# Reordering the opening of a projection and attention kernel

## The reference

```python
def _layernorm(x, axis=-1, eps=1e-05):
    return (x - mean(x)) / sqrt(var(x) + eps)

x = x + attention(_layernorm(x), Wq, Wk, Wv, Wo, bo)   # causal softmax, scores * HEAD ** -0.5
x = x + int8_matmul(_layernorm(x), rhs)                # both factors rounded to int8 by their absmax
```

## Time and profile before

| | |
|---|---|
| time, median of 3 | 1675.17 us (1672.59 to 1675.41) |
| the profiled execution's own time | 1670.0 us |
| its span, first to last instruction | 1668.2 us |
| PE, DVE, ACT, POOL busy | 94%, 91%, 82%, 17% of the span |
| `project` works from | about 5.6 to 231.7 us |

### The profile page before, as it was taken

How to read it: one execution, slowest core, us unless ns; L and a number is a source line. 1 busy time by engine, 2 the same in 40 slices (tenths; PEclk the granted TensorE clock), 3 DMA queues, 4 the chain that set the end, 5 groups by cost and what they waited for, 6 DMA issues and landing times.

```text
span 1668.2 us, 40684 instructions
## 1 busy us (share of the span) xinstructions
PE 1562.9 (94%) x16715; PEld 623.8 (37%) x16715; DVE 1522.0 (91%) x1839; ACT 1362.6 (82%) x2659; POOL 290.9 (17%) x397
## 2 busy tenths in 40 slices
PE   4799989999999999999999999999999999999965
PEld 2444433333333333333333333333333333344433
DVE  5589889999999999999999999999999999578876
ACT  3355559999999999999999999999999999877651
POOL 5343401211111111111121111120202020100120
PEclk9899999999999999999999999999999999999986
DMA  2454320101121212111111212121212142034532
GB/s 82 141 161 144 124 65 17 51 18 51 43 63 43 63 52 55 57 50 60 47 60 47 60 47 59 47 61 52 62 51 63 48 119 78 15 116 134 154 118 70
DMA packets 105613, 118.79 MB, mean 71 GB/s; under 512 B 20688, under 2 KB 87508, under 8 KB 105428
## 3 DMA queue, kind: packets, MB, share of 16 engines
q1 hardware_dynamic: 105428, 116.19, 23.4%
HBM read 66.81 MB, written 48.76 MB: 69 GB/s over the span
## 4 chain that ended last, share of the span: by engine, by line
DVE 54%; PE 27%; DMA 1%; ACT 1%; issue 1%; SPq 1%; POOL 0%; ACTq 0%; DVEq 0%
DVE pmax L355 46%; PE psum L1155 12%; PE psum L1136 6%; DVE pblk L355 4%; PE psum L263 3%; PE psum L1196 3%; PE psum L277 2%; PE psum L282 2%; DMA f_rs<-inverse_sums 1%; DVE V L1438 1%; ACT prob L1326 1%; DVE V L1457 1%; DVE V L1445 1%; PE psum L1220 1%; DVE f_amax L1463 1%
## 5 line engine op out<-in xcount | busy, mean ns | idle before, releaser
L1326 ACT ACTIVATE prob<-psum 128x512 f32<-128x512 f32 (+1 forms) x2304 | 1180.9, 574 | 136.4 <-PE psum L1136 113.0
L355 DVE TENSOR_REDUCE pmax<-psum 128x2 f32<-128x1024 f32 (+1 forms) x960 | 1100.9, 1216 | 12.7 <-PE psum L282 6.6
L1155 PE MATMUL psum<-prob,V 128*32 128x256 f32 x8704 | 675.7, 391 | 0.0
L1136 PE MATMUL psum<-Q,K 50*128 50x512 f16 (+3 forms) x2560 | 465.1, 350 | 3.8 <-ACT prob L1326 1.0
L1392 POOL TENSOR_SCALAR_AFFINE_SELECT prob<-prob 128x512 f32<-128x512 f32 x256 | 160.6, 640 | 1177.6 <-ACT prob L1326 1175.1
L263 PE MATMUL psum<-K,Q 48*128 48x512 f16 x1536 | 298.4, 384 | 20.3 <-DVE pmax L355 19.4
L1155 PEld LDWEIGHTS psum<-prob,V 128*32 128x32 f32 x8704 | 181.4, 108 | 294.1 <-issue 213.8
L1136 PEld LDWEIGHTS psum<-Q,K 50*128 50x128 f16 x2560 | 174.7, 94 | 251.5 <-ACT prob L1326 185.1
L263 PEld LDWEIGHTS psum<-K,Q 48*128 48x128 f16 x1536 | 74.3, 93 | 265.8 <-DVE pmax L355 219.7
L355 DVE TENSOR_REDUCE pblk<-psum 128x8 f32<-128x1024 f32 x128 | 151.8, 1219 | 5.9 <-PE psum L282 5.7
L282 PE MATMUL psum<-K,Q 48*128 48x512 f16 (+3 forms) x1024 | 129.0, 299 | 0.0
(11 more groups left out here) (122 smaller groups left out, 709.4 us busy)
## 6 DMA issues: line engine op xcount, KB each, us to landing
f_x<-in_L_attn_x SPq DMA_DIRECT2D x32, 512.0 KB, 4.0
unnormalised<-ust SPq DMA_DIRECT2D x64, 256.0 KB, 2.9
q_parts<-part SPq DMA_DIRECT2D x64, 128.0 KB
k_parts<-part SPq DMA_DIRECT2D x64, 128.0 KB
Q<-q_parts SPq DMA_DIRECT2D x128, 64.0 KB, 2.5
K<-k_parts SPq DMA_DIRECT2D x128, 64.0 KB, 2.0
out<-V SPq DMA_DIRECT2D x16, 512.0 KB, 3.3
f_rs<-inverse_sums SPq DMA_DIRECT2D x28, 256.0 KB
```

The costliest lines, as they stand in the source:

```text
L355: nc.vector.tensor_reduce(to, of, axis=AX.X, op=ALU.max).then_inc(M.mx_free, 1)
L1136: m = nc.tensor.matmul(PS[:, SB + i % RING, at:at + n], K[it % 2][rows, pair, kb * P:(kb + 1) * P], Q[it % 2][rows, pair, (c + 1) * CH - n ...
L1155: m = nc.tensor.matmul(PS[32 * h:32 * h + 32, UB, to:to + n], V[:, it // NG * NT + kb, col:col + 32], prob[(it * NSTEP + k) % PRING][:, h, ...
L1326: nc.scalar.activation(prob[g % PRING][:, h, 0:n], PS[:, SB + i % RING, 0:n], ACT.Exp, scale=by).then_inc(exp_done, 1)
```

## The change

`constants` is no block any more: it is called at the head of POOL's program in `project`, and its users wait for its semaphore `c_done` (ACT for 1, DVE for 2, PE for all 12). The rest reorders `project`:

- SP: Wv gets its own semaphore. The load of chunk n + 3 now stands in iteration n behind that chunk's stores and ahead of its `load_attention`; before, it stood in iteration n + 1, behind them. Chunk 2 is loaded in iteration 0 as before.
- POOL: the constants come first. `constant_rows(A.K[0])` moves ahead of `low_rows(1)`.
- DVE: `scale_weights` waits for Wq and Wk only. `scale_value_weight` moves from ahead of chunk 0's low parts to behind them.
- ACT: `take_xT(0)` moves ahead of `root(1)`. The copy of Wv's split weight moves from ahead of chunk 0's high parts to behind `take_xT(1)`.
- PE: the spreading of the powers comes ahead of `transpose(0)`, the first turn of Wv behind it. The turn back moves from between Q and K of chunk 0 to behind `transpose(1)`.

```diff
-        constants(nc, identf, identb, identh, maskid, mask, eps)
@@ SP
-            for t, src in zip(w, (Wq, Wk, Wv)):
-                sp.dma_start(t[:], src.rearrange("(k p) n -> p k n", p=P)).then_inc(w_in, 16)
+            for t, src, there in zip(w, (Wq, Wk, Wv), (w_in, w_in, wv_in)):
+                sp.dma_start(t[:], src.rearrange("(k p) n -> p k n", p=P)).then_inc(there, 16)
             load(1)
             for n in range(NC):
-                if n + 2 < NC:
-                    sp.wait_ge(xn_ready, 2 * n + 2)
-                    load(n + 2)
+                if n == 0:
+                    sp.wait_ge(xn_ready, 2)
+                    load(2)
                 (stores of chunk n)
+                if n + 3 < NC:
+                    sp.wait_ge(xn_ready, 2 * n + 4)
+                    load(n + 3)
                 (load_attention)
@@ POOL
+            constants(nc, pool, identf, identb, identh, maskid, mask, eps, c_set, c_done)
             low_rows(0)
-            low_rows(1)
-            pool.wait_ge(xl_ready, 4)
+            pool.wait_ge(xl_ready, 2)
             constant_rows(A.K[0])
             pool.wait_ge(fixed, 2)
+            low_rows(1)
@@ DVE
-                dve.wait_ge(w_in, 48)
+                dve.wait_ge(w_in, 32)
+                dve.wait_ge(c_done, 2)
                 nc.vector.tensor_scalar(gdiag[:], identf[0:2, 0:2], gpow[:, 0:1], None,
             normalise(1)
-            scale_value_weight()
             for n in range(NC):
                 low_part(n, 3)
+                if n == 0:
+                    scale_value_weight()
                 if n + 2 < NC:
                     statistics(n + 2)
@@ ACT
+            act.wait_ge(c_done, 1)
             root(0)
             for half in range(2):
                 high_rows(0, half)
+            take_xT(0)
             root(1)
-            take_xT(0)
             for half in range(2):
                 high_rows(1, half)
-            act.wait_ge(vT_back, 1)
-            nc.scalar.copy(wp[2][:].rearrange("p i k c -> p (i k c)"), ...
             for n in range(NC):
                 if n + 1 < NC:
                     take_xT(n + 1)
+                    if n == 0:
+                        act.wait_ge(vT_back, 1)
+                        nc.scalar.copy(wp[2][:].rearrange("p i k c -> p (i k c)"), ...
@@ PE
+            pe.wait_ge(c_done, 12)
             pe.wait_ge(wmax_ready, 1)
             nc.tensor.transpose(PS[0:2, 7, 0:P], wmax[:], identf[:]).then_inc(wmaxT, 1)
-            value_weight(False)
-            transpose(0)
             pe.wait_ge(pow_ready, 1)
             nc.tensor.matmul(PS[:, 7, 256:258], ones2[:], gdiag[:], start=True, stop=True).then_inc(pow_spread, 1)
+            transpose(0)
+            pe.wait_ge(wv_in, 16)
+            value_weight(False)
-                    if n == 0 and j == 1:
-                        value_weight(True)
                 if n + 1 < NC:
                     transpose(n + 1)
+                if n == 0:
+                    value_weight(True)
```

More of the change, by code:

```diff
@@ L182, in build @@
             M = max_pass_buffers(nc, inner)
-            project(nc, x_t, Wq, Wk, Wv, qk_d, PS, identf, identh, maskid, mask, eps, scale, A, M, F)
+            project(nc, x_t, Wq, Wk, Wv, qk_d, PS, identf, identb, identh, maskid, mask, eps, scale, A, M, F)
             attend(nc, x_t, qk_d, u_d, r_d, o_d, out_t, PS, identf, identb, identh, maskid, mask, eps, scale, Wo, bo, Wf, A, M, F)
@@ L451, in store_group @@
         sp.dma_start(o_d[gi * G:(gi + 1) * G, :, cols], F.group_u[rows, :]).then_inc(F.group_out, 16)
[L454 to L479, removed]
@@ L482, in project, with constants @@
-def project(nc, x_t, Wq, Wk, Wv, qk_d, PS, identf, identh, maskid, mask, eps, scale, A, M, F):
+def constants(nc, pool, identf, identb, identh, maskid, mask, eps, c_set, c_done):
+    nc.gpsimd.memset(eps[:], EPS).then_inc(c_done, 1)
+    for m in (identf, identh, identb, maskid, mask):
+        nc.gpsimd.memset(m[:], 0.0).then_inc(c_set, 1)
+    for k, m in enumerate((identf, identh, identb)):
+        pool.wait_ge(c_set, k + 1)
+        nc.gpsimd.affine_select(out=m[:], in_=m[:], compare_op=ALU.not_equal, fill=1.0, base=0,
+                                pattern=[[-1, P]], channel_multiplier=1).then_inc(c_done, 1)
+    pool.wait_ge(c_set, 5)
+    for half in range(2):
+        rows = slice(half * HALF, (half + 1) * HALF)
+        pool.wait_ge(c_done, 4 + 4 * half)
+        for i in range(2):
+            nc.gpsimd.affine_select(out=maskid[rows, i, :], in_=maskid[rows, i, :],
+                                    compare_op=ALU.not_equal, fill=1.0, base=i * HALF,
+                                    pattern=[[-1, P]], channel_multiplier=1).then_inc(c_done, 1)
+            nc.gpsimd.affine_select(out=mask[rows, i, :], in_=mask[rows, i, :], compare_op=ALU.is_ge,
+                                    fill=NEG, base=i * HALF, pattern=[[-1, P]],
+                                    channel_multiplier=1).then_inc(c_done, 1)
+    pool.wait_ge(c_done, 12)
@@ L483, in project @@
+def project(nc, x_t, Wq, Wk, Wv, qk_d, PS, identf, identb, identh, maskid, mask, eps, scale, A, M, F):
     ctx = ExitStack()
@@ L512, in project @@
         winv = sb("winv_qk", [P, 2])
+        c_set, c_done = sem("c_set"), sem("c_done")
         w_in = sem("w_in")
+        wv_in = sem("wv_in")
         x_in = [sem(f"x_in{s}") for s in range(2)]
@@ L806, in _ @@
                 high_rows(0, half)
+            take_xT(0)
             root(1)
-            take_xT(0)
             for half in range(2):
                 high_rows(1, half)
-            act.wait_ge(vT_back, 1)
-            nc.scalar.copy(wp[2][:].rearrange("p i k c -> p (i k c)"),
-                           PS[:, 7, :].bitcast(F16)).then_inc(wv_ready, 1)
             for n in range(NC):
@@ L824, in _ @@
                     take_xT(n + 1)
+                    if n == 0:
+                        act.wait_ge(vT_back, 1)
+                        nc.scalar.copy(wp[2][:].rearrange("p i k c -> p (i k c)"),
+                                       PS[:, 7, :].bitcast(F16)).then_inc(wv_ready, 1)
                 else:
```

## The result

The changed kernel takes 1662.09 us in the median of 4 runs (1661.84 to 1664.65), the kernel before 1674.31 beside it. The medians are 12.2 us apart. The ratio taken over the runs is 0.9937, interval 0.9922 to 0.9952: 8 to 13 us faster, where 10.5 were forecast. In a second series the medians were 1661.98 and 1672.15, 10.2 us apart, with a ratio of 0.9934 (0.9919 to 0.9950).

The account below looks back on a forecast made before the run. Bound: VectorE's reductions of maxima and PE's matmuls, with the opening's gain handed on whole. 2.3 + 7.15 = 9.45 us with slow V, 11.25 without; 10.5 taken: 1675.2 - 10.5 = 1664.7 us, range 1658 to 1670.2.

Parts of the forecast that it names:

- Loads first: Start: SP's first DMA goes from 5.65 to 0.8, 4.85 us earlier; waits on `c_done` cost nothing.
- K[0]'s memsets: Opening, POOL: two pieces of 3.5 us make DVE's weight scaling wait; some 4 of 4.85 us are lost again.
- the race: Whether `gdiag`, at 10.94, gets in before POOL's first K[0] memset, about level with it; if it loses, all ends at 24.9.
- The rival without a wait: Opening: a memset does not hold DVE up; gain 15.0 to 16.8 us, time about 1659; chance 0.24 (13 to 18).
- The prediction's rule for every `tensor_scalar`: DVE: a plain SBUF-to-SBUF `tensor_scalar` waits until the POOL instruction under way is over.
- The move of Wv's scaling has thus only changed what waits: Chunk 0: Wv's scaling, now behind the low parts, ends at 31.7; V starts at 33.5, against 34.48 before.
- Slow clock in chunk 0: PE pauses about 4 us behind `transpose(1)`, so V of chunk 0 takes about 4.6 us in place of 2.78: +1.8.
- a rival: Chunk 2: PE's clock drops there too, costing 4 us; gain 6.5, time 1668.5; chance 0.14 (5 to 8.5).
- Late loads: SP: `load(3)` and `load(4)`, issued near 32 and 48, come in time; DVE's waits of 6.49 and 4.64 us go.
- the 2.3: First stall: K[1]'s memsets still hold POOL; `high_rows(3)` comes at 51.7 in place of 54.01, gain 2.3 of 6.5 us.
- 7.15 us: Chunk 2's stretch: falls from 19.63 to a steady 12.48, including the 4.64 of waiting and the slow clock after it.
- the forecast's band: Whole kernel: the forecast counts as met with a gain of 8.5 to 13 us; chance 0.52.

Follow-up runs that it names:

- the run with the other order: Changed kernel with ACT's two waits before the first root swapped, so the table load waits for eps, not the variance: 1661.37 us, ratio 0.9926.
- the run in pieces: Changed kernel with each of the two memsets of K[0] cut in eight, at the same place: 1657.51 us, ratio 0.991.
- K[1]'s memsets late: Changed kernel with K[1]'s two memsets moved on POOL from behind low_rows(2) to behind low_rows(3) and low_rows(4), one each: 1669.11 us, ratio 0.9978.

## Why the prediction was right, and where it was off

**Loads first: right, and one term missed.** The first load is at 0.80, the first statistics at 4.66. The waits on `c_done` were costed at nothing. Their time is nothing, but with ACT's ahead of the variance's the table load comes behind the variance: 1.28 us on the path, shown by the run with the other order.

**K[0]'s memsets: right.** The wait was taken in full and came in full; `gdiag` lost the race. `normalise(1)` ended at 25.5, where 24.1 was forecast with the race won and 24.9 with it lost; the table load's 1.28 us more than cover the 0.6 left. The rival without a wait is refuted by the run in pieces. The prediction's rule for every `tensor_scalar` was too wide: L704, above, did not wait. The Trainium skill, page "SBUF — State Buffer", section "SBUF: two separate sides", has this as an exclusive lock for the whole instruction: the 3.52 us of `gdiag` agree. But L737, with Wv in its old places, waited 3.72 us, through three POOL instructions in a row (two L622 and two V memsets stood there, L737 began inside the second L622), and was not let in between them. Elsewhere, as at 25.93 and 29.49 with K[0]'s memsets in their old place, DVE came in between two.

**"The move of Wv's scaling has thus only changed what waits": wrong.** V of chunk 0 came at 35.2, near its old 34.48, where 33.5 was forecast. But the step compared with the old kernel, where two small instructions of the scaling waited some 0.9 us each (L736 took 1.00 us, L739 1.08). With all other edits made and Wv in its old places they wait 4.1 together, the scaling ends at 32.8 in place of 29.9, K of chunk 0 takes 4.95 in place of 2.75, and V starts at 39.4. The move is worth 5.8 us beside the others, and the loads 4.0 in place of 9.45.

**Slow clock in chunk 0: right.** 4.6 us were expected for V, 5.00 came; filling the pauses gave 2.79 and a clock of 1.00, so the pauses were the cause. Chunk 1 came 2.9 later than before where 0.8 was forecast: 1.7 more from the late start of V and 0.4 more from its length. The slow clock did not reach chunk 2, as a rival had it: the stretches 42.15 to 50.85 and 50.85 to 65.32 stand at 1.00.

**Late loads: right in the profile, mis-sized as a cause.** Both waits are gone. Yet with the old place of the loads one of them would have gone anyway, since chunk 1 comes later in the new order. K[1]'s memsets take the place of the first wait as forecast: `high_rows(3)` at 53.61, gain 0.4 in place of 2.3, because all that leads there was later. At the start of chunk 2's stretch the gain was 2.6, near the 2.3. For the stretch itself I counted 7.15 us; 5.2 came, for the wait for K[1] lies in that very stretch (14.47 against 12.48), and without it the stretch takes 12.04 (K[1]'s memsets late). That is the term that was mis-sized: the two, summed 9.45, measured 7.7 at chunk 3, which came at 65.32 where near 63 was forecast.

**The sum.** 10.5 was taken between 9.45 and 11.25, but the slow V that goes with 9.45 came. The opening gave 7.7 to 8.3, below the 8.5 at which the forecast's band starts; the medians say 10 to 12. That they agree with 10.5 is in part luck: 2 to 4 us of them arise behind the mark, where the prediction put nothing, and their cause stays open. Undoing one part at a time costs 4.0, 5.6, 5.8 and -0.3, together 15 for a whole of 8.3: each part is worth that only while the others are in place. ACT's and PE's remaining moves were not undone singly.

## What to carry to other kernels

Idle time in a profile says what is late next, not what its removal gives: ask what comes in its place, as K[1]'s memsets did. When a long POOL instruction is moved, look for `tensor_scalar` instructions of DVE from SBUF to SBUF in its new company, however small (2x2 elements waited here, 2x1 did not), and cut it in pieces if there are any. When an opening gets faster, look at the queue that issues the loads again: here a load belonged ahead of the stores once the chunks came earlier. And before a small gain is believed, run the same kernel twice and see how far its marks lie apart.

## What was unexpected

An instruction on four elements lasted 3.52 us, and cutting the memset beside it in eight, with no less work, brought the mark 5.6 us forward. The order of two waits in ACT's program moved the table load from 0.97 to 6.56. And 29 matmuls that compute nothing made the opening 1.5 us shorter.
